# Reordering the start of a token mixer: the second group's layer norm and difference, and the first group's level 0 operands, moved in two engines' programs

## The reference, cut to what matters

```python
x = x + mixer(_layernorm(x))
# mixer(x):
shifted = pad(x, one token)[:, :T]
delta = shifted - x
z = tanh((x + delta * mu_x) @ W_x1.T).reshape(B, T, 5, lr)
mus = einsum('blnr,dnr->blnd', z, W_x2) + x_bias       # r, w, k, v, g
r = (x + delta * r_mu) @ W_r.T                          # and k, v, g alike
w = tanh((x + delta * w_mu) @ A_w.T) @ B_w.T + b_w
w = -exp(w)
# per head, over tokens:  o_t = q_t (S + u kv);  S = exp(w_t) S + kv
o = group_norm(o) * silu(g)
return o @ W_o.T
```

## Time and profile before

| | |
|---|---|
| time before, median of 3 runs | 1426.53 us (1425.16 to 1426.65) |
| profiled execution, its own time | 1413.66 us |
| profiled execution, span of the core | 1411.8 us |
| mean granted TensorE clock | 0.978 of full speed |
| busy: PE, DVE, POOL, ACT | 92%, 66%, 53%, 44% |

### The profile page before, as it was taken

How to read it: one execution, slowest core, us unless ns; L and a number is a source line. 1 busy time by engine, 2 the same in 40 slices (tenths; PEclk the granted TensorE clock), 3 DMA queues, 4 the chain that set the end, 5 groups by cost and what they waited for, 6 DMA issues and landing times.

```text
span 1411.8 us, 30933 instructions
## 1 busy us (share of the span) xinstructions
PE 1304.2 (92%) x9852; PEld 881.0 (62%) x9853; DVE 934.9 (66%) x1964; ACT 620.8 (44%) x1519; POOL 746.7 (53%) x1080
## 2 busy tenths in 40 slices
PE   5799998999869999999999999999979999999996
PEld 3466655665646666666666666666645666666664
DVE  2577887778647788888888888888873322222221
ACT  2455545554514555555555555555543122222221
POOL 5124542345425687778777787778744222222222
PEclk9899999999979999999999999999989999999998
DMA  5998000000136544545455545455423222222221
GB/s 148 282 318 239 7 1 1 0 1 1 24 39 100 104 113 123 125 125 123 124 128 127 122 111 125 122 124 129 112 71 72 43 47 45 45 45 45 45 41 23
DMA packets 152749, 127.80 MB, mean 91 GB/s; under 512 B 41630, under 2 KB 145510, under 8 KB 152614
## 3 DMA queue, kind: packets, MB, share of 16 engines
q1 hardware_dynamic: 140310, 112.02, 32.1%
q0 software_dynamic: 12304, 14.10, 6.4%
HBM read 35.90 MB, written 44.83 MB: 57 GB/s over the span
## 4 chain that ended last, share of the span: by engine, by line
PE 57%; DVE 7%; issue 3%; ACT 2%; DMA 0%; POOL 0%; DVEq 0%; SPq 0%; ACTq 0%; POOLq 0%
PE bank_st L2182 11%; PE bank_v L2200 7%; PE bank_v L2010 6%; PE bank_s L2022 5%; PE bank_st L2032 5%; PE bank_o L2052 5%; PE bank_m L1985 4%; PE bank_s L2182 3%; DVE neg_raw L1714 3%; PE bank_st L2041 3%; PE bank_m L2074 3%; DVE bank_st L1725 2%; PE bank_o L2191 2%; PE bank_m L2062 1%; PE bank_v L2000 1%
## 5 line engine op out<-in xcount | busy, mean ns | idle before, releaser
L1714 DVE TENSOR_REDUCE neg_raw<-bank_s 100x2 f32<-100x722 f32 x256 | 229.1, 895 | 9.2 <-PE bank_s L2022 9.2
L1573 ACT ACTIVATE prob<-bank_st 120x400 f32<-120x400 f32 (+1 forms) x384 | 166.2, 513 | 153.0 <-PE bank_st L2041 153.0
L1513 POOL DMA_INDIRECT out<-lead_shared,target x57 | 88.4, 1550 | 234.2 <-DVE lead_shared L1929 185.8
L1725 DVE TENSOR_SCALAR bank_st<-bank_st 121x1200 f32<-121x1200 f32 x128 | 180.4, 1409 | 1.3 <-PE bank_st L2032 0.8
L1924 DVE TENSOR_TENSOR lead_shared<-silu,bank_st 128x512 f32<-128x512 f32 x57 | 39.2, 688 | 193.0 <-PE bank_st L2182 193.0
L2182 PE MATMUL bank_st<-expert_w,lead_shared 128*128 x344 | 159.6, 600 | 0.7 <-issue 0.5
L564 ACT ACTIVATE q_heads<-q 32x192 f32<-32x192 f32 (+3 forms) x224 | 82.6, 369 | 139.0 <-DVE q L749 134.7
L1418 POOL TENSOR_TENSOR neg_diag<-xident_b,neg_max 100x400 bf16<-100x400 bf16 x128 | 109.5, 855 | 39.9 <-DVE neg_max L1719 39.2
L983 PE MATMUL bank_l<-q_heads,k 128*100 128x192 f32 (+4 forms) x512 | 114.8, 366 | 14.7 <-ACT q_heads L564 7.9
L396 POOL TENSOR_TENSOR mixed<-part,xn_t 128x400 f32<-128x400 f32 x80 | 84.4, 1080 | 82.5 <-DVE part L690 82.4
L1670 ACT ACTIVATE lead_shared<-bank_o 128x512 f32<-128x512 f32 x57 | 34.0, 597 | 196.5 <-PE bank_o L2191 196.5
(11 more groups left out here) (263 smaller groups left out, 2676.3 us busy)
## 6 DMA issues: line engine op xcount, KB each, us to landing
slot_rows<-empty SPq DMA_DIRECT2D x9, 2967.0 KB, 25.9
k_st<-k_part SPq DMA_DIRECT2D x252, 90.2 KB
lead_shared<-k_part SPq DMA_DIRECT2D x132, 90.2 KB
lead_shared<-in_ctx_t SPq DMA_DIRECT2D x32, 270.8 KB
expert_w<-in_w SPq DMA_DIRECT2D x16, 512.0 KB, 4.5
rows<-slot_rows SPq DMA_DIRECT2D x57, 129.0 KB, 2.1
q_st<-q_part SPq DMA_DIRECT2D x126, 50.0 KB, 3.1
residual<-in_w SPq DMA_DIRECT2D x16, 256.0 KB, 4.6
```

The costliest lines, as they stand in the source:

```text
L1573: act.activation(prob[0:KEYS[c], t % 2, c], bank_st[0:KEYS[c], c, 0:4 * T], ACT.Exp).then_inc(exp_done, 1)
L1714: dve.tensor_reduce(neg_raw[:, h:h + 2], bank_s[0:T, :, 0:S], AX.X, ALU.max, negate=True).then_inc(max_done, 1)
L1725: dve.tensor_scalar(tile, tile, CLAMP, -CLAMP, ALU.min, ALU.max).then_inc(clipped, 1)
```

## The change

Nothing is added or taken out; instructions of ACT and DVE move within their own programs. POOL, PE and SP keep theirs.

- ACT: `heads(0, 0, 0)` (level 0 operands of group 0) moves from behind piece 7 to ahead of piece 6. `norm_apply(1)` moves from there to ahead of piece 7 (the readings of the gates). `front(1, 1, 0)` (the copies to `xn_t`) moves into the first body, behind `heads` of level 1.
- DVE: `norm_stats(1)` moves from behind piece 7 of group 0 to ahead of it. `front(1, 1, 1)` (`delta` and `xz`) moves into the first body, behind the collection of level 0.

```diff
@@ ACT @@
+                if piece == 6:
+                    heads(0, 0, 0)
+                if piece == 7:
+                    norm_apply(1)
                 front(0, 0, piece)
-            heads(0, 0, 0)
-            norm_apply(1)
-            front(1, 1, 0)
...
+                    if s == 0 and first:
+                        front(1, 1, 0)
                     if s == 2 and not first:
                         turned(g - 1)
@@ DVE @@
+                if piece == 7:
+                    norm_stats(1)
                 front(0, 0, piece)
-            norm_stats(1)
-            front(1, 1, 1)
...
+                    if s == 0 and first:
+                        front(1, 1, 1)
                     if s == 1 and not first:
                         head_scale(g - 1)
```

## The result

| | median | runs | ratio to before (95% interval) |
|---|---|---|---|
| before | 1426.59 us | 1425.16 to 1427.57 (4) | |
| changed | 1416.61 us | 1416.15 to 1416.87 (4) | 0.9934 (0.9921 to 0.9947) |
| changed, timed again | 1415.62 us | 1415.48 to 1415.77 (5) | 0.9932 (0.9918 to 0.9945) |

The medians differ by 9.98 us where 10.0 was forecast; by the ratio it is 9.4 us (7.6 to 11.3). The second timing stands against 15 runs of the kernel before on the same chip, median 1426.04 us. The profiled execution of the changed kernel has an own time of 1416.62 us, at the median of its runs, and not 1403.7; why, the run of the kernel before again shows.

A forecast was written before the change was run, and what follows sets the result against it. PE, busy 92%, was held by a 7.61 us hole before group 1's transposes and the low clock after it. Gains of 7.45 and 2.55 us sum to 10.0, giving 1416.5 us, range 1414.3 to 1420.4.

The forecast's parts named there:

- Statistics ahead of the gates: On DVE, group 1's statistics start at 33.7 instead of 41.34, beside POOL's last mixed; offset is there at 37.6.
- Heads ahead of the rate: On ACT, four level 0 heads run from 32.27 to 34.85, ahead of rate, and cost nothing.
- First term: On PE, group 1's transposes start at 40.05 instead of 47.49, a gain of 7.45 us.
- Second term: On PE, from transposes to group 1's w_x1 products takes 7.15 us instead of 9.70, a gain of 2.55 us.
- The wait for `xz`: New PE wait of about 1.4 us ahead of group 1's w_x1 products, behind level 1.
- The sum: Gains of 7.45 and 2.55 us up to group 1's w_x1 products give 10.0 us; forecast time 1416.5 us, chance 0.79.
- Nothing is given back: Behind group 1's w_x1 start all runs as before, only earlier; rival: half given back in first bodies, 1421.5 us, chance 0.05.
- The own time of the profile: The changed kernel's profiled execution was to take 1403.7 us, from 1413.66 less 10.0.
- The fallen clock, the first rival: Short PE waits around 40 to 47 us halve the clock; gain 7.45 us alone, 1419.1 us, chance 0.09.
- Slower, the last rival: Each us of offset after 37.8 delays transposes and levels alike; 1431.5 us if 5 us beyond 47.8; chance 0.03.
- The range: Whole-kernel time from 1414.3 us up to 1420.4 us, reaching to the fallen-clock case with scatter.

The follow-up runs named there:

- the run of the kernel before again: The kernel before, unchanged, profiled a second time; own time 1425.18 us.
- the run with the heads behind: Changed kernel with the four level 0 heads put back behind the gate readings on ACT; ratio 0.9968 to the kernel before.
- hole filled: Kernel before with ten idle products on PE between the gate products and group 1's transposes; ratio 1.0000 to the kernel before.
- early norm, difference ahead: Changed kernel with the xn_t copies, delta and xz put back ahead of the first body; ratio 0.9958 to the kernel before.
- the run with the norm made later: Changed kernel with twelve idle statistics on DVE ahead of the second group's norm; ratio 0.9979 to the kernel before.

## Why the prediction was right, step by step

- *Statistics ahead of the gates.* Right. Forecast 33.7, found 34.14 in an execution that came to this place 0.49 us later (37.52 against 37.03). `mixed` and the statistics ran beside each other and took what they took before, 1.88 and 1.40 us.
- *Heads ahead of the rate.* Right that they cost nothing there; the run with the heads behind shows what they cost otherwise, 4.4 us of stretch.
- *First term, 7.45.* From gate products to transposes it was 10.46 us in both profiles of before and is 2.90 now: 7.56.
- *Second term, 2.55.* From transposes to `w_x1` it was 9.70 and 8.13 and is 7.08: 2.62 in the first profile, 1.05 in the other. The mechanism was right, but I took one execution's size for a constant: the moment at which the clock comes back varies. The wait for `xz` is 1.11, not 1.4.
- *The sum, 10.0.* That the medians differ by 9.98 is partly luck. The term came from the profile with the longer low clock; from the other it would have been 8.13 - 7.15 = 0.98 and the sum 8.4, and the measured 7.6 to 11.3 holds both.
- *What the second term is made of.* I didn't separate it. With the clock at 1.00 throughout, the old order has a stretch of 17.96, the early norm with the early heads 11.13, the whole change 9.98: 6.83 us for norm and heads, 1.15 for the difference behind level 0. In the two profiles the old clock cost 0.6 and 2.2 us on top. The early norm and the late difference also depend on each other: no gain of the difference's place is seen without the early norm, and with it, it is 2.5 us, since PE then waits 0.37 us in level 0 rather than 2.79, and the clock stays.
- *Nothing is given back.* Against the second profile of before, the three profiles of the changed kernel are ahead by 9.36, 8.51 and 8.97 us when the `w_x1` products start (47.50, 48.35 and 47.89 against 56.86), and by 8.56, 9.05 and 9.41 in own time (1416.62, 1416.13 and 1415.77 against 1425.18): 8.9 and 9.0 on average. Single executions differ by up to 0.8 us behind this place, so a loss of a few tenths could not be seen.
- *The own time of the profile.* 1403.7 was wrong by 13 us, because the first profile was of an execution that lacked twelve pairs of waits in the attention stage. The median, from which I took the same us, was not touched by that.
- *The fallen clock, the first rival.* Not here: waits of 0.37, 0.22 and 1.11 us, and a clock of 1.00 in all profiles of the changed kernel. But it is close by: after one wait of 2.05 us (hole filled), 2.79 (early norm, difference ahead) or 3.02 (heads behind) the clock fell. The Trainium skill, TensorE: Matmul & The Clock Gate, section "A second HAM failure mode: psum-queue depth-cycling", tells of a clock that goes back and forth in a kernel with many brief stops. In this stretch no run shows that: in these three kernels the clock fell once, behind a single longer wait, and the brief waits of the changed one left it at 1.00.
- *Slower, the last rival.* It priced each us of a late `offset` at one us. The run with the norm made later shows 6.25 us for 3.80, so that price was too low.
- *The range.* Its upper end, 1420.4, doesn't follow from its own words: 1419.1 and the 0.8 us of scatter that the lower end carries are 1419.9. Nothing hangs on it here.

## What to carry to other kernels

At the start of a software-pipelined kernel, look for work whose input is long there but which stands in its engine's program behind work of the stage that just drains. When it is brought forward, walk through each engine's queue again: what was hidden in the old hole (here the heads) is on the path once the hole is closed, and the order behind the hole (here the difference), of which no gain was seen before, begins to count. Compare stretches of the same profile rather than whole times where an execution can differ by ten us elsewhere, and take more than one profile before pricing a low clock.

## What the runs showed of the hardware

The moment at which TensorE's clock rises varies between executions of one program, after the hole (3.8 and 9 us after the transposes begin) and at the very start. The `w_x1` products of group 0, in the first profile of before and in the second:

```profile
15.79 4.50 PE L922 MATMUL bank_f<-xz,w_x 128*128 128x400 f32 x8 [2.91 <-DVE xz L714]
```

```profile
15.83 5.70 PE L922 MATMUL bank_f<-xz,w_x 128*128 128x400 f32 x8 [2.91 <-DVE xz L714]
```

This 1.2 us is why the gate products start at 37.0 in one execution and at 38.3 in another. The granted clock is listed as 1.00 from 0 us on in both, although these products, the last ones of the first profile apart, follow each other at 0.67 us where later ones take 0.34, so at half the pace; the pace of the rows, not the listed clock, tells the level there. The Trainium skill, TensorE: Matmul & The Clock Gate, section "What's actually happening", says that the number of slow products at a start varies from run to run; the trace agrees, with about five of the eight slow in the first profile and all eight in the second.

The scatter of whole times goes with the granted clock too. Of 21 runs of the kernel before on one chip, the four shortest (1422.23 to 1422.55 us) had a mean clock of 0.982 or 0.983 and the four longest (1426.76 to 1427.55) one of 0.974 or 0.975. In which stage they lost it isn't shown.
